# A convolution attention and a quantized FFN on one core: four engines' instruction lists in another order

## The reference

```
q   = layernorm(x)                        # over the last axis, 256
kv  = k[b,h,i,:] * k[b,h,j,:]             # k = v = ctx, 16 heads of 8 channels, all pairs (i, j)
y   = causal_convolution(kv, ssm_kernel[h]) + kv * D[h]
x1  = x + sum_i y[b,i,j,h,:] * q[b,h,i,:]
f   = layernorm(x1)
out = x1 + down(silu(gate(f)) * up(f))    # gate, up: 256 -> 704, down: 704 -> 256
```

## Time and profile before

| | |
|---|---|
| median of three runs | 76.36 us (76.27 to 76.8) |
| span of the profiled execution | 74.5 us |
| median less span | 1.86 us |
| TensorE busy | 69.8 us, 94% |
| VectorE busy | 61.7 us, 83% |
| POOL busy | 58.8 us, 79% |
| ScalarE busy | 45.5 us, 61% |
| loads and stores | 8.29 MB |

### The profile page before, as it was taken

The page is one execution under the profiler, slowest core; times in us unless marked ns, Lnnn a source line. Parts: engine busy times, 40 slices in busy tenths (PEclk is TensorE's granted clock), DMA queues, the critical chain, the costliest instruction groups (busy, mean ns, idle before and its releaser), DMA issues.

```text
span 74.5 us, 1494 instructions
## 1 busy us (share of the span) xinstructions
PE 69.8 (94%) x470; PEld 57.7 (77%) x470; DVE 61.7 (83%) x187; ACT 45.5 (61%) x115; POOL 58.8 (79%) x76
## 2 busy tenths in 40 slices
PE   5999989999999989999999999999999999999920
PEld 4666557988878848889798889797999989899810
DVE  0078899999988999999999899999968884586760
ACT  1503436464867879967746894657768796776400
POOL 6033587997999999899999999479998999339230
PEclk9999999999999999999999999999999999999998
DMA  0898999999997000000000000000002006000404
GB/s 8 235 254 230 372 315 364 324 382 392 361 356 224 29 0 0 0 0 4 9 0 0 0 0 4 0 0 0 0 13 70 0 0 210 1 9 0 140 1 141
DMA packets 7128, 8.29 MB, mean 111 GB/s; under 512 B 816, under 2 KB 6224, under 8 KB 7120
## 3 DMA queue, kind: packets, MB, share of 16 engines
q1 hardware_dynamic: 6768, 7.88, 33.0%
q10 hardware_dynamic: 352, 0.31, 1.2%
HBM read 7.12 MB, written 1.07 MB: 110 GB/s over the span
## 4 chain that ended last, share of the span: by engine, by line
PE 68%; POOL 16%; DVE 9%; issue 2%; ACT 1%; POOLq 0%; DVEq 0%
PE conv L1018 26%; PE down L1037 13%; POOL products L387 10%; PE conv L985 6%; PE turn L1058 5%; PE conv L994 5%; PE conv L996 5%; POOL rstd_q L371 4%; PE turn L965 3%; DVE terms L731 3%; PE turn L947 2%; PE turn L1037 2%; POOL terms L279 2%; DVE terms L734 1%; DVE terms L738 1%
## 5 line engine op out<-in xcount | busy, mean ns | idle before, releaser
L1018 PE MATMUL conv<-f_parts,wgu 128*128 128x256 f16 x176 | 22.1, 273 | 0.0
L387 POOL TENSOR_TENSOR products<-k_skip 128x512 f32<-128x512 f32 (+1 forms) x16 | 18.2, 1147 | 1.2 <-DMA k_skip<-ctx_skip 1.2
L1018 PEld LDWEIGHTS conv<-f_parts,wgu 128*128 128x128 f16 x176 | 16.6, 98 | 2.7 <-DVE hidden L746 0.2
L257 POOL TENSOR_TENSOR h_lo<-hidden,h_hi 128x256 fp32r<-128x256 f32 x18 | 13.1, 745 | 2.6 <-ACT h_hi L527 2.5
L746 DVE SCALAR_TENSOR_TENSOR hidden<-conv,su_sb,gate_act 128x256 f32<-128x256 f32 (+1 forms) x24 | 11.5, 482 | 3.0 <-ACT gate_act L522 2.8
L522 ACT ACTIVATE gate_act<-conv,sg_sb 128x256 f32<-128x256 f32 (+1 forms) x24 | 11.2, 467 | 4.2 <-PE conv L1018 3.9
L985 PE MATMUL conv<-products,toeplitz 128*128 128x288 f32 x32 | 11.3, 437 | 0.1
L731 DVE TENSOR_TENSOR terms<-conv,q_ext 128x512 f32<-128x512 f32 x16 | 10.9, 682 | 0.5 <-ACT q_ext L504 0.3
L994 PE MATMUL conv<-products,toeplitz 128*128 128x288 f32 x32 | 10.6, 413 | 0.3 <-DVE toeplitz L664 0.3
L996 PE MATMUL conv<-products,toeplitz 128*128 128x288 f32 x32 | 10.4, 406 | 0.0
L527 ACT ACTIVATE h_hi<-hidden 128x256 fp32r<-128x256 f32 x20 | 8.3, 413 | 3.4 <-DVE hidden L746 3.1
(11 more groups left out here) (64 smaller groups left out, 121.6 us busy)
## 6 DMA issues: line engine op xcount, KB each, us to landing
k_skip<-ctx_skip SPq DMA_DIRECT2D x3, 384.0 KB, 5.9
toeplitz<-taps_pad SPq DMA_DIRECT2D x2, 512.0 KB, 8.6
out<-x_sb SPq DMA_DIRECT2D x7, 128.0 KB, 1.7
toeplitz<-matrices SPq DMA_DIRECT2D x3, 256.0 KB, 5.4
wg_int<-wg_t SPq DMA_DIRECT2D x1, 704.0 KB, 7.6
wu_int<-wu_t SPq DMA_DIRECT2D x1, 704.0 KB, 8.8
wd_int<-wd_t SPq DMA_DIRECT2D x1, 640.0 KB, 10.0
x_sb<-x SPq DMA_DIRECT2D x1, 512.0 KB, 5.1
```

The source lines that it names most:

```text
L257: eng.tensor_tensor(low_of(i, t), hidden[up_lanes(t), i % 2, t, :], high_of(i, t), ALU.subtract).then_inc(done, 1)
L387: nc.gpsimd.tensor_tensor(view(products[:, n:n + 1], first * MADE + GROUP, [[MADE, halves], [GROUP, 4], [1, GROUP]]), view(k, 0, [[EXT * B ...
L1018: done = nc.tensor.matmul(bank_of(i, t)[:, n, :], wgu[:, c, column:column + P], f_parts[:, i % 2, part, c, :], start=(c == 0 and part == 0 ...
```

## The change

The lists of TensorE, VectorE, ScalarE and POOL are put in another order; each has the same steps as before. Waits for loads, which stood between the steps, now stand in the helpers of the steps that need them, so that they move along. `wait(eng, sem, n)` becomes `eng.wait_ge(sem, n)` where n is never 0, which is the same instruction. SyncE's list is not touched. The helpers that got a wait:

```diff
+        def wait_for_k(eng, n):
+            first = [0, 1, 2, 4, 8, 12]
+            if n in first:
+                eng.wait_ge(k_loaded[first.index(n)], 16)
...
             def root_q(t):
+                if t == 0:
+                    pool.wait_ge(half_ready, 1)
+                pool.wait_ge(q_variance, t + 1)
...
             def pairs(n, first, last):
+                if first == 0:
+                    wait_for_k(pool, n)
...
             def direct(n):
+                if n == 0:
+                    dve.wait_ge(anti_ready, 1)
+                if n < 2 or n % 2 == 0:
+                    dve.wait_ge(direct_loaded[n if n < 2 else n // 2 + 1], 16)
```

The same is done in `squares`, `gate`, `all_products`, `stats_of_q`, `hidden_units`, `turn_q` (for `ident_ready`), `gates` (for `w_ready`) and `add_skip_to_taps`. The lists, cut to the stretches of which the prediction speaks. POOL:

```diff
             root_q(0)
-            pool.wait_ge(k_loaded[2], 16)
+            root_q(1)
             pairs(2, 0, 1)
             pairs(2, 1, 2)
-            root_q(1)
             pairs(3, 0, 1)
             pairs(3, 1, 2)
+            pairs(4, 0, 2)
             root_q(2)
...
             pairs(7, 0, 2)
+            root_q(4)
+            pairs(8, 0, 2)
             root_f(0)
-            pool.wait_ge(k_loaded[4], 16)
-            pairs(8, 0, 2)
             merge_front(nc.gpsimd, 2)
-            root_q(4)
             pairs(9, 0, 2)
             root_f(1)
             pairs(10, 0, 2)
             root_q(5)
+            merge_front(nc.gpsimd, 3)
+            root_q(6)
             pairs(11, 0, 2)
-            pool.wait_ge(k_loaded[5], 16)
             pairs(12, 0, 2)
-            root_q(6)
-            merge_front(nc.gpsimd, 3)
-            root_q(7)
+            pairs(13, 0, 2)
             merge_front(nc.gpsimd, 4)
             low(0, 0)
+            low(0, 1)
+            root_q(7)
             root_f(2)
```

TensorE:

```diff
             convolve_within(2)
+            turn_q(1, q_ready, 1)
             convolve_across(3)
-            turn_q(1, q_ready, 1)
             convolve_within(3)
             sum_terms(0, q_ready, 0)
             convolve_across(4)
-            turn_q(2, q_ready, 2)
             convolve_within(4)
             convolve_across(5)
+            convolve_across(6)
+            turn_q(2, q_ready, 2)
             convolve_within(5)
             sum_terms(1, x1_ready, 1)
-            convolve_across(6)
-            convolve_within(6)
             turn_q(3, q_ready, 3)
             convolve_across(7)
+            convolve_within(6)
             convolve_within(7)
             sum_terms(2, x1_ready, 2)
...
             convolve(10)
+            gates(0, 0)
             turn_q(5, q_ready, 5)
-            pe.wait_ge(w_ready, 1)
-            gates(0, 0)
             gates(0, 1)
+            sum_terms(3, f_ready, 2)
             convolve(11)
-            sum_terms(3, f_ready, 2)
             gates(0, 2)
```

More of the change, by code:

```diff
@@ L783, in _ @@
+            direct(1)
+            all_products(1, 1, 2)
             multiply_terms(0)
-            variance_of_q(1)
-            dve.wait_ge(direct_loaded[2], 16)
+            shift_of_q(1)
             direct(2)
             direct(3)
-            dve.wait_ge(x_loaded[2], 16)
+            multiply_terms(1)
             stats_of_q(2)
-            shift_of_q(1)
+            stats_of_q(3)
             moments_of_q(2)
-            multiply_terms(1)
-            variance_of_q(2)
-            stats_of_q(3)
@@ L795, in _ @@
-            dve.wait_ge(direct_loaded[3], 16)
             direct(4)
             direct(5)
+            variance_of_q(2)
+            multiply_terms(2)
             shift_of_q(2)
-            moments_of_q(3)
-            multiply_terms(2)
-            variance_of_q(3)
             multiply_terms(3)
             add_sum(0)
-            dve.wait_ge(x_loaded[3], 16)
+            moments_of_q(3)
             stats_of_q(4)
             stats_of_f(0)
+            variance_of_q(3)
+            direct(6)
@@ L831, in _ @@
             shift_of_f(1)
-            moments_of_q(7)
-            variance_of_q(5)
-            stats_of_f(2)
             multiply_terms(7)
+            variance_of_q(6)
+            shift_of_q(5)
             low_f(0)
-            shift_of_q(5)
-            variance_of_q(6)
             multiply_terms(8)
@@ L841, in _ @@
             merge_back(dve, 3)
+            shift_of_q(6)
+            merge_last(dve, 3)
             multiply_terms(9)
-            variance_of_q(7)
-            merge_last(dve, 3)
-            merge_back(dve, 4)
-            dve.wait_ge(scales_loaded, 3 * 16)
-            hidden_units(0, 0)
-            shift_of_q(6)
-            hidden_units(0, 1)
-            moments_of_f(2)
-            add_sum(3)
-            variance_of_f(2)
-            stats_of_f(3)
+            stats_of_f(2)
+            moments_of_q(7)
@@ L854, in _ @@
+            add_sum(3)
+            moments_of_f(2)
+            hidden_units(0, 0)
+            merge_back(dve, 4)
+            stats_of_f(3)
+            hidden_units(0, 1)
+            merge_last(dve, 4)
+            variance_of_f(2)
+            moments_of_f(3)
+            variance_of_q(7)
+            hidden_units(0, 2)
             multiply_terms(10)
-            moments_of_f(3)
             shift_of_f(2)
             variance_of_f(3)
-            hidden_units(0, 2)
-            merge_last(dve, 4)
@@ L860, in _ @@
             multiply_terms(11)
+            hidden_units(0, 3)
+            shift_of_f(3)
+            shift_of_q(7)
             add_sum(4)
-            hidden_units(0, 3)
+            multiply_terms(12)
+            low_f(2)
             stats_of_f(4)
-            shift_of_f(3)
             hidden_units(0, 4)
-            low_f(2)
-            multiply_terms(12)
+            hidden_units(0, 5)
+            moments_of_f(4)
             low_f(3)
-            moments_of_f(4)
-            shift_of_q(7)
+            merge_last(dve, 5)
@@ L871, in _ @@
             variance_of_f(4)
             multiply_terms(13)
-            merge_last(dve, 5)
+            add_sum(5)
             shift_of_f(4)
-            hidden_units(0, 5)
+            stats_of_f(5)
             hidden_units(1, 0)
-            add_sum(5)
+            moments_of_f(5)
             multiply_terms(14)
-            stats_of_f(5)
+            multiply_terms(15)
+            variance_of_f(5)
             hidden_units(1, 1)
-            moments_of_f(5)
-            low_f(4)
             merge_last(dve, 6)
@@ L924, in _ @@
             scale_out(2, 1)
+            low(3, 1)
             hidden_units(3, 4)
@@ L1137, in _ @@
             turn_f(6, x1_ready, 8)
+            gates(2, 3)
             gates(2, 4)
+            turn_f(7, f_ready, 7)
             downs(2, 0)
-            turn_f(7, f_ready, 7)
+            downs(2, 1)
             gates(2, 5)
-            downs(2, 1)
-            downs(2, 2)
             gates(3, 0)
             gates(3, 1)
+            downs(2, 2)
             gates(3, 2)
```

302 lines of the change are left out of this document (146 added, 156 removed).

## The result

The changed kernel takes 80.76 us (median of 4 runs, 80.71 to 81.4), the kernel before 76.55 on the same chip (four runs, with the three that gave 76.36): a ratio of 1.0573, 95% interval 1.0517 to 1.0628. I had forecast 75.9 with a range to 77.6. The profiled execution took 81.4 with a span of 79.6 (the other three: 78.9 to 79.0), 5.1 more than before.

The account below looks back on a forecast made before the run. TensorE was taken as the bound, with gains only in its holes: 0.18 + 0.57 = 0.75, less 0.1 for groups and 0.2 for a held merge, gives 0.45 us. Forecast 75.9 us, range 75.1 to 77.6.

Parts of the forecast that it names:

- Nothing until 8.8 us: Start: first transposes come some 0.1 earlier, but all ends at the toeplitz load landing at 8.76; nothing gained.
- 0.18 gained from 8.8 to 12.7: Direct(2) earlier wins 0.04 at 9.86; across(3) and turn_q(1) find pairs(3) and norm_q(1) ready; together 0.18.
- Turn_f(1)'s wait gone, 0.57: 12.5 to 26.5: low_f(0) comes earlier, so turn_f(1)'s wait of 0.51 and 0.06 of slow restart go.
- Merge_back(2) beside merge_front(2), 0.2 lost: From 21.4, VectorE's merge holds POOL's merge_front(2), so sum_terms(2), wanted at 22.25, loses 0.2.
- My upper bound, 0.47: Loss at merge_back(2) if VectorE is the one that waits for POOL's merge_front(2); 0.2 was taken.
- 27 to 66: Same work dealt out in another order on a full TensorE: nothing won; only group costs.
- 0.1 for groups: Down projection cut into 13 groups instead of 10: costs between 0 and 0.3, taken as 0.1.
- the second rival: VectorE's merge_back(3), merge_last(3) wait 1.1 and 1.2 behind POOL's pairs(11), pairs(12): 78.1 us, about 77.2 if one; chance 0.18.
- The forecast without a merge loss: Whole kernel: 0.75 gained less 0.1 for groups, leaving out the 0.2 for the held merge.
- Tail at no cost: Low(3, 1) and add(2, 0) come 0.35 to 0.7 later, still before TensorE wants them; tail's waits remain.
- Chances: Whole kernel: faster (below 75.6) 0.33, same 0.44, slower (above 77.12) 0.23, from the second rival and part of the third.

Follow-up runs that it names:

- The probe: Kernel's computation left out; POOL multiplies two SBUF tiles or only writes, VectorE does single instructions beside it; executed once, VectorE's two-operand instruction ended 0.54 after POOL's.
- the old order with one collision: Kernel before with POOL's merge_front(3) and root_q(6) moved ahead of pairs(11) and pairs(12): 77.09 us, ratio 1.0107.

## Why the prediction was wrong

| Two SBUF operands on VectorE in | changed order | old order | difference |
|---|---|---|---|
| merges, directs, lows (whole kernels) | 80.76 | 76.55 | 4.21 |
| directs, lows | 77.98 | 75.83 | 2.15 |
| nothing | 76.05 | 75.53 | 0.52 |

So 3.7 of the 4.2 us are VectorE and POOL locking each other out: 2.1 at the merges, 1.6 at directs and lows (differences of medians; each row is from one chip, the chips 0.4% apart). That is shown, by taking the lock away in both orders, with statistics of about the same length in the same places. It is a net sum: the old order was held too and gets about 0.7 faster (75.53 against 76.22), the changed one about 4.6 (ratios 1.0573 and 0.9975). The probe and the old order with one collision (0.95 longer, 0.7 lost) show the mechanism itself. The Trainium skill ("SBUF — State Buffer", Who interferes with whom) has the rule, that VectorE with two SBUF inputs and a GpSimd instruction that reads SBUF exclude each other, and that the loser fully blocks; the traces agree from both sides (VectorE 0.5 to 1.1 longer, POOL 0.3 to 0.5).

Point by point:

- **Nothing until 8.8 us:** right; where the load lands sets convolve_across(2) here too (idle 0.60 for it, start 9.79).
- **0.18 gained from 8.8 to 12.7:** wrong. Direct(2) and (3) collide with pairs(3), which the change lets start earlier, and take 1.18 for 0.60. I had counted POOL's earlier pairs as a gain only.
- **Turn_f(1)'s wait gone, 0.57:** the wait went, as forecast, though turn_f(1) starts at 27.59 and not below 26.9. But taken away alone it was worth 0.08 of time (76.25 for 76.33, inside the interval): VectorE has the next convolve's terms to finish at the same time as ever. And it was itself the mark of a collision, which I didn't see: POOL's root_q(4), held by merge_back(2), kept shift_of_q(4) for 0.44. In the old order with statistics for merges the wait is gone too.
- **Merge_back(2) beside merge_front(2), 0.2 lost:** the place was right, the side wrong. POOL wasn't held, VectorE was, by 0.47, and TensorE waited 0.41. My upper bound, 0.47, was the answer. I took the lesser value because in the rows it was POOL that was held; but in both rows VectorE had been first, so they could not speak for the other case.
- **27 to 66, "the same work is only dealt out in another order on a full TensorE: nothing won", 0.1 for groups:** this is the step that failed: it took every instruction at its old length, whatever now runs beside it. TensorE waits 2.96 us there (0.84, 0.69, 1.08 and 0.35) instead of losing 0.1. VectorE was busy for 22.16 of 22.60 up to 50.00, nearly as tight as TensorE, so most of what its instructions grow by reaches TensorE (waits of 3.4 us for 5.3 us of growth over the whole kernel). Merge_back(3), merge_last(3), merge_last(5), low(0, 5), merge_last(7) and others grew. I listed this as the second rival, for merges of one tile alone, and gave it 0.18. There it was nearly right: pairs(11) started 0.19 ahead of merge_back(3), as my list had it (0.2), and VectorE waited 1.85 against 2.3 (1.1 and 1.2; the 2.7 in my sum, and with it the 78.1, don't follow from them: they give 77.9), TensorE 1.53. It should have been asked of every VectorE instruction with two SBUF operands in the new lists, the directs and lows too.
- **The order's own cost:** without any collision the changed order is 0.52 slower than the old one. The forecast without a merge loss had it 0.65 faster, but 0.57 of that was turn_f(1)'s wait, which the old order without collisions doesn't have either (26.49, above). So some 0.6 remains between the 0.1 gained that was forecast and the 0.52 lost. The changed order is 0.27 ahead at convolve_within(2) (9.49 for 9.76), still 0.25 at gates(0, 2), where both have done the same work (31.78 for 32.03), and 0.49 behind at the last gates (66.45 for 65.96), so 0.74 is lost between. The wait of 0.33 ahead of gates(2, 2) for hidden_units(2, 1) is nearly half of it. The rest (cut groups of downs are the candidate) wasn't isolated and stays open.
- **Tail at no cost:** wrong by a little: it costs 0.25 alone.
- **Chances:** I gave 0.23 to slower, because I asked where the change removes waits and priced only two places where the lists newly meet. Rival two's own number ended at 78.1, 2.7 short: the direction was among my rivals, the size in none.

No version of the changed order with the whole computation beats the old one. The edit taken from it that moves only VectorE's statistics ties.

## What to carry to other kernels

Where two engines can lock each other out, a list isn't an order of one engine: go through all pairs of VectorE instructions with two SBUF operands (by the probe also copies and tensor_scalars) and POOL instructions that read SBUF, see who comes upon whom, and price each meeting by the rest of the running instruction. Look at VectorE's busy time against the stage before calling an edit on it free, and look for such waits as long instructions, since no idle time shows them. Keeping the two apart by waits on POOL gained at most 0.4 of 4.2 here, part of it perhaps by the tail's order, and in one run lost 0.6. What removed the conflict was an operand in PSUM, or statistics in place of work with two operands. Work with one operand alone doesn't do it: the copy was held.

## What was not expected of the hardware

- A VectorE copy and a tensor_scalar of one SBUF tile were held beside POOL as well (1.21, against 0.45 for the copy beside a POOL memset), while statistics with one SBUF operand were not (0.67 to 0.69).
- Merges of the kernel before that came upon a running root of POOL (one column, 0.55 long) were not held. POOL's root_q(6) there, upon which merge_back(3) came at 28.69 and took 0.68:

```profile
28.47 0.56 POOL L371 TENSOR_TENSOR rstd_q<-variance_q,minus_half 128x1 f32<-128x1 f32 x1
```

  The same holds at 35.69 (root from 35.47, merge 0.68) and 54.17 (root from 54.02, merge 0.69). By the rule as the prediction cites it, a lock for the whole instruction, each of them would have waited for the root to end. So a meeting with a root costs VectorE nothing, one with a POOL instruction over a large tile does. A root that came second was held all the same (1.04 in the earlier trace rows).
- Two VectorE instructions in a row don't keep POOL out: POOL's slips in between, and the second waits (1.75 at 15.54 in the probe).
- SyncE went on from its wait for toeplitz 2 and 3 at anything between 7.69 and 9.67 us in the profiled executions, though its list of loads is the same in all. In the latest of them VectorE waited 0.34 and TensorE 0.60 for that load.
